# Router logits as seven differences to expert 7, with a PSUM bank of its own for each group of a tile

## What is computed

```
logits = (h @ router_w.T + router_b).reshape(T, O, E)        # T=4096, O=512, E=8
probs = softmax(logits, axis=-1)
w, sel = top_k(probs, 2);  w = w / sum(w)
c[t, e] += w summed over the features o for which sel picks e   # .at[t_idx, sel].add(w)
expert_out = einsum('th,eoh->teo', h, expert_w) + expert_b
final = einsum('te,teo->to', c, expert_out)
x = x + final
```

## Time and profile before

| | |
|---|---|
| median of 3 runs | 2307.93 us (2307.9 to 2308.26) |
| span of the profiled execution, from its first to its last instruction | 2306.4 us |
| PE busy | 2285.2 us, 99% |
| DVE busy | 1682.9 us, 73% |
| ACT busy | 1145.2 us, 50% |
| POOL busy | 11.3 us |
| last tile's groups to the first matmul of the second expert tile | 1583.8 to 1628.3 us |

### The profile page before, as it was taken

The page is one execution under the profiler, slowest core; times in us unless marked ns, Lnnn a source line. Parts: engine busy times, 40 slices in busy tenths (PEclk is TensorE's granted clock), DMA queues, the critical chain, the costliest instruction groups (busy, mean ns, idle before and its releaser), DMA issues.

```text
span 2306.4 us, 29968 instructions
## 1 busy us (share of the span) xinstructions
PE 2285.2 (99%) x10201; PEld 1881.0 (82%) x10201; DVE 1682.9 (73%) x2522; ACT 1145.2 (50%) x1686; POOL 11.3 (0%) x20
## 2 busy tenths in 40 slices
PE   7999999999999999999999999999999999999999
PEld 5777888888888887888888888888888888888887
DVE  8985444444434346888899999998988888888883
ACT  7754333232323235788888888888422222222221
POOL 0000000000000000000000000000000000000000
PEclk9999999999999999999999999999999999999999
DMA  6314212122121317211111212115322222222220
GB/s 206 105 42 139 76 37 75 55 56 75 37 86 26 91 37 255 73 57 66 59 64 64 78 55 77 61 58 199 134 96 82 77 95 79 80 95 76 83 82 23
DMA packets 154026, 191.04 MB, mean 83 GB/s; under 512 B 62898, under 2 KB 96242, under 8 KB 151666
## 3 DMA queue, kind: packets, MB, share of 16 engines
q1 hardware_dynamic: 110690, 135.26, 18.1%
q10 hardware_dynamic: 43152, 55.06, 7.3%
q0 software_dynamic: 128, 0.07, 0.0%
HBM read 129.01 MB, written 61.34 MB: 83 GB/s over the span
## 4 chain that ended last, share of the span: by engine, by line
PE 89%; issue 5%; DVE 4%; ACT 2%; DMA 0%; ACTq 0%; POOLq 0%; POOL 0%; DVEq 0%; SPq 0%
PE slot L1599 16%; PE plane L1749 10%; PE plane L1747 10%; PE plane L1745 10%; PE ex L1785 10%; PE ex L1787 10%; PE ex L1786 10%; PE pj L1612 7%; PE slot L1661 3%; PE slot L1568 1%; PE slot L1650 1%; DVE cols L1238 1%; DVE ew_lo L1478 1%; ACT x1t_hi L795 0%; PE slot L1578 0%
## 5 line engine op out<-in xcount | busy, mean ns | idle before, releaser
L1599 PE MATMUL slot<-y_hi,wgu 128*128 128x512 f32 x1024 | 402.6, 393 | 1.4 <-DVE y_lo L1118 0.7
L1599 PE MATMUL slot<-y_lo,wgu 128*128 128x512 f32 x1024 | 399.8, 390 | 0.0
L1745 PE MATMUL plane<-rw_hi,hb 128*128 128x512 f32 x1008 | 392.2, 389 | 0.0
L1749 PE MATMUL plane<-rw_lo,hb 128*128 128x512 f32 x1008 | 392.1, 389 | 0.0
L1747 PE MATMUL plane<-rw_hi,hb 128*128 128x512 f32 x1008 | 392.1, 389 | 0.0
L1785 PE MATMUL ex<-ew_hi,hb 128*128 128x512 f32 x992 | 386.0, 389 | 0.2 <-ACT ex L1056 0.2
L1787 PE MATMUL ex<-ew_lo,hb 128*128 128x512 f32 x992 | 385.9, 389 | 0.0
L1786 PE MATMUL ex<-ew_hi,hb 128*128 128x512 f32 x992 | 385.9, 389 | 0.0
L1056 ACT ACTIVATE ex<-eb_sb 128x512 f32<-128x512 f32 x248 | 149.0, 602 | 448.9 <-DVE acc L1507 385.8
L1453 DVE SCALAR_TENSOR_TENSOR lead_in<-code_in,wts 128x1024 bf16<-128x1024 bf16 x256 | 311.4, 1216 | 1.2
L1599 PEld LDWEIGHTS slot<-y_hi,wgu 128*128 128x128 f32 x1024 | 192.8, 188 | 45.5 <-DVE q_scale L1125 2.9
(11 more groups left out here) (164 smaller groups left out, 3213.6 us busy)
## 6 DMA issues: line engine op xcount, KB each, us to landing
hb<-h_scratch SPq DMA_DIRECT2D x34, 512.0 KB, 3.3
code_scratch<-half_code SPq DMA_DIRECT2D x64, 256.0 KB, 2.0
half_in<-code_scratch SPq DMA_DIRECT2D x32, 512.0 KB, 3.4
hb<-h_scratch ACTq DMA_DIRECT2D x30, 512.0 KB, 3.7
h_scratch<-ht ACTq DMA_DIRECT2D x48, 256.0 KB, 2.9
q_raw<-in_w_ffn SPq DMA_DIRECT2D x21, 512.0 KB, 3.5
x_scratch<-x_res ACTq DMA_DIRECT2D x8, 1024.0 KB, 4.3
rraw<-in_rwT SPq DMA_DIRECT2D x8, 1024.0 KB, 9.2
```

The source lines that it names most:

```text
L1599: last = mm(slot[s % 2][:, g, :], wgu[:, c, r * P:(r + 1) * P], y[:, c, :], start=(c == 0 and v == 0), stop=(c == DC - 1 and v == 1))
L1745: mm(bank[:, :, :], hb[:, u, c, 0, :], rw_hi[:, w, c, o], start=False, stop=False, skip_group_check=True)
L1749: last = mm(bank[:, :, :], hb[:, u, c, 0, :], rw_lo[:, w, c, o], start=False, stop=True, skip_group_check=True)
```

## The change

The router's weights and biases become differences: plane q holds expert `LOADED[q]` minus expert 7. The eighth logit is then zero and is neither multiplied, nor evacuated, nor stored.

- GpSimd makes the seven difference planes in the middle blocks of stage 1 (`gaps`): 28 steps, each a DMA in, a subtraction of 128x512, and a DMA out to `gap_dram`, five steps after each `power(i)`; and the bias differences in three instructions before `power(7)`. SP loads the seven planes from `gap_dram` once all 28 are out.
- A tile has `PT = 7` groups. Groups 0 to 2 and 4 to 6 are pairs of planes for a half; group 3 is the seventh plane with both halves in one bank. Each group has its own bank (`plane` 0 to 3, `spare` 0 to 2), seeded for the next tile right after its evacuation.
- `half` now works on planes 1 to 6 in pairs of three, and takes the seventh plane (`side`) and zero in with `scalar_tensor_tensor`: 14 steps (`KT`) for 12. Its first steps for s = 0 wait for three evacuations, the fifth for the fourth. The last subtraction is one instruction over seven planes. `stand` takes the sign of seven planes and, in a second instruction, that of minus the second logit.
- Between the stages, raw experts 6 and 7 are loaded as soon as SP is past tile 29; the last tile's groups go in the order `LAST_GROUPS`, the splits in the order `SPLITS`; ACT's list has `stand(30, 1)` before the first `split_expert`; expert 7's high part takes the place of raw expert 6, so its split waits for `elo` of expert 6. One `split_router` and one router load fall away.

```diff
...
-PT = 8
-KT = 12
+PT = 7
+KT = 14
 KD = 2
 EPS = 1.1920928955078125e-07
 SCALE_FLOOR = 1.0011717677116394e-08
 
 
+NQ = E - 1
+LOADED = [0, 1, 4, 5, 2, 6, 3, 7]
+HOME = [(1, 3), (4, 6), (3, 7)]
+SIDE = [0, 7]
+PLACES = [[3, 0, 1, 2, 4, 5, 6, 7], [0, 1, 2, 4, 5, 6, 3, 7]]
+
 UW = 2 * D
 STEP = [128.0, 32.0, 8.0, 2.0]
+LAST_GROUPS = [0, 4, 1, 5, 2, 6, 3]
+SPLITS = [0, 1, 2, 3, 6, 4, 5, 7]
...
+            sp.wait_ge(gap_out, 16 * NQ * DC)
             sp.dma_start(bias_sb[:, :, :, :], rb).then_inc(braw_in, 16)
             sp.wait_ge(drained, use(NBLK - 1, f"gu{HC - 1}")[0] + 1)
-            for e in range(E):
-                sp.dma_start(rraw[:, e, :, :].rearrange("p c o -> p (c o)"), rwT[e]).then_inc(rraw_in[e], 16)
+            for e in range(NQ):
+                sp.dma_start(rraw[:, e, :, :].rearrange("p c o -> p (c o)"), gap_dram[e]).then_inc(rraw_in[e], 16)
...
+            load_expert(6)
+            load_expert(7)
             sp.wait_ge(plane_filled, (NT - 1) * PT)
             load_h(0, 0)
-            for b in range(4):
+            for b in range(3):
                 sp.wait_ge(plane_filled, (NT - 1) * PT + 2 * (b + 1))
-                for e in (2 * b, 2 * b + 1):
-                    sp.dma_start(eraw[:, e, :, :].rearrange("p c o -> p (c o)"), ewT[e]).then_inc(eraw_in[e], 16)
+                load_expert(2 * b)
+                load_expert(2 * b + 1)
...
+            def gaps(count):
+
+                for t in range(step[0], min(step[0] + count, NQ * DC)):
+                    c, q = t // NQ, t % NQ
+                    at = slice(c * D, (c + 1) * D)
+                    if q == 0:
+                        if c:
+                            pool.wait_ge(gap_done, t)
+                        pool.dma_start(ref_rows, rwT[NQ][:, at]).then_inc(gap_ref, 16)
+                    if t:
+                        pool.wait_ge(gap_out, 16 * t)
+                    pool.dma_start(rows, rwT[q][:, at]).then_inc(gap_in, 16)
+                    pool.wait_ge(gap_ref, 16 * (c + 1))
+                    pool.wait_ge(gap_in, 16 * (t + 1))
+                    nc.gpsimd.tensor_tensor(rows, rows, ref_rows, ALU.subtract).then_inc(gap_done, 1)
+                    pool.wait_ge(gap_done, t + 1)
+                    pool.dma_start(gap_dram[q][:, at], rows).then_inc(gap_out, 16)
+                step[0] += count
+
             power(0)
-            with pool.Fori(1, NBLK - 1) as i:
+            for i in range(1, NBLK - 1):
                 power(i)
+                gaps(5)
+            pool.wait_ge(braw_in, 16)
+            ref_bias = bias_sb[:, PT, :, :]
+            for s in range(2):
+                at = bias_sb[:, 4 * s:4 * s + 3, :, :].rearrange("p b e n -> p (b e) n")
+                nc.gpsimd.tensor_tensor(at, at, ref_bias[:, s, :].unsqueeze(1).to_broadcast([P, 6, HO]),
+                                        ALU.subtract).then_inc(bias_gap, 1)
+            nc.gpsimd.tensor_tensor(bias_sb[:, 3, :, :], bias_sb[:, 3, :, :], ref_bias, ALU.subtract).then_inc(bias_gap, 1)
...
+            act.wait_ge(drained, l1_use(NBLK - 1, "h1")[0] + 1)
+            for g in range(4, PT):
+                seed(g)
...
+            def evacuate(n, s, u):
+
+                for g in range(4 * s, 4 if s == 0 else PT):
+                    act.wait_ge(plane_filled, n * PT + (g + 1))
+                    nc.scalar.activation(logits_at(g, u), bank_of(g)[:, :, :], ACT.Copy).then_inc(evac, 1)
+                    act.wait_ge(evac, n * PT + (g + 1))
+                    seed(g)
...
+            def stand(n, s, u, second=None):
 
                 act.wait_ge(tour, n * (2 * KT) + (s + 1) * KT)
                 if not isinstance(n, int) or n * 2 + s > 1:
                     act.wait_ge(joined, n * 2 + (s - 1))
-                flat = L[:, s, :, :].rearrange("p e n -> p (e n)")
-                nc.scalar.activation(sgn[:, s, :], flat, ACT.Sign).then_inc(signs, 1)
-                act.wait_ge(signs, n * 2 + (s + 1))
+                flat = L[:, s, u:u + NQ, :].rearrange("p e n -> p (e n)")
+                second = m2[:, s, :] if second is None else second
+                nc.scalar.activation(sgn[:, s, 0:NQ * HO], flat, ACT.Sign).then_inc(signs, 1)
+                nc.scalar.activation(sgn[:, s, NQ * HO:E * HO], second, ACT.Sign, scale=-1.0).then_inc(signs, 1)
+                act.wait_ge(signs, n * 4 + 2 * (s + 1))
...
+                if e == E - 1:
+                    act.wait_ge(elo, SPLITS.index(6) + 1)
+                nc.scalar.activation(ew_hi(e), raw_expert(e), ACT.Copy).then_inc(ehi, 1)
+
+            evacuate_last(0)
+            stand(NT - 2, 1, 0)
+            evacuate_last(1)
             split_expert(0)
+            evacuate_last(2)
             split_expert(1)
-            stand(NT - 2, 1)
-            evacuate_last(0, 2)
-            evacuate_last(0, 3)
-            evacuate_last(1, 0)
-            evacuate_last(1, 1)
+            evacuate_last(3)
+            evacuate_last(4)
             split_expert(2)
-            evacuate_last(1, 2)
-            split_expert(3)
-            evacuate_last(1, 3)
-            for e in range(4, E):
+            evacuate_last(5)
+            evacuate_last(6)
+            for e in SPLITS[3:]:
                 split_expert(e)
-            stand(NT - 1, 0)
+            stand(NT - 1, 0, 1)
...
 
-                dve.wait_ge(evac, n * PT + 4 * (s + 1))
-                step(tt(top4, L[:, s, 0:4, :], L[:, s, 4:8, :], ALU.max))
-                step(tt(low4, L[:, s, 0:4, :], L[:, s, 4:8, :], ALU.min))
+                last = isinstance(n, int) and n == NT - 1
+                dve.wait_ge(evac, n * PT + (PT if s else LAST_GROUPS.index(2) + 1 if last else 3))
+                step(tt(top3, L[:, s, 1:4, :], L[:, s, 4:7, :], ALU.max))
+                step(tt(low3, L[:, s, 1:4, :], L[:, s, 4:7, :], ALU.min))
                 after(1)
-                step(tt(top2, top4[:, 0:2, :], top4[:, 2:4, :], ALU.max))
+                step(tt(top2[:, 0, :], top3[:, 0, :], top3[:, 2, :], ALU.max))
                 after(2)
-                step(tt(low4[:, 0:2, :], low4[:, 0:2, :], low4[:, 2:4, :], ALU.max))
-                step(tt(top4[:, 0:2, :], top4[:, 0:2, :], top4[:, 2:4, :], ALU.min))
+                step(tt(low3[:, 0, :], low3[:, 0, :], low3[:, 2, :], ALU.max))
+                if s == 0:
+                    dve.wait_ge(evac, n * PT + (LAST_GROUPS.index(3) + 1 if last else 4))
+                step(stt(top2[:, 1, :], side, 0.0, top3[:, 1, :], ALU.max, ALU.max))
+                step(stt(low3[:, 1, :], side, 0.0, low3[:, 1, :], ALU.min, ALU.max))
                 after(3)
+                step(tt(top3[:, 0, :], top3[:, 0, :], top3[:, 2, :], ALU.min))
+                after(5)
+                step(stt(top3[:, 1, :], side, 0.0, top3[:, 1, :], ALU.max, ALU.min))
                 step(tt(m1, top2[:, 0, :], top2[:, 1, :], ALU.max))
-                after(5)
-                step(tt(low4[:, 0:2, :], low4[:, 0:2, :], top4[:, 0:2, :], ALU.max))
                 step(tt(m2, top2[:, 0, :], top2[:, 1, :], ALU.min))
-                after(7)
-                step(tt(low4[:, 0, :], low4[:, 0, :], low4[:, 1, :], ALU.max))
-                after(9)
-                step(tt(m2, m2, low4[:, 0, :], ALU.max))
+                after(8)
+                step(tt(low3[:, 0:2, :], low3[:, 0:2, :], top3[:, 0:2, :], ALU.max))
+                after(11)
+                step(tt(low3[:, 0, :], low3[:, 0, :], low3[:, 1, :], ALU.max))
+                after(12)
+                step(tt(m2, m2, low3[:, 0, :], ALU.max))
                 if joins:
                     join(n if s else n - 1, 1 - s)
-                after(10)
-                step(tt(L[:, s, 0:4, :], L[:, s, 0:4, :], m2.unsqueeze(1).to_broadcast([P, 4, HO]), ALU.subtract))
-                step(tt(L[:, s, 4:8, :], L[:, s, 4:8, :], m2.unsqueeze(1).to_broadcast([P, 4, HO]), ALU.subtract))
+                after(13)
+                step(tt(L[:, s, u:u + NQ, :], L[:, s, u:u + NQ, :], m2.unsqueeze(1).to_broadcast([P, NQ, HO]), ALU.subtract))
...
-            for b in range(4):
-                group(NT - 1, 1, NT // 2 - 1, 0, b)
-                group(NT - 1, 1, NT // 2 - 1, 1, b, bank=spare[b])
+            for g in LAST_GROUPS:
+                group(NT - 1, 1, NT // 2 - 1, g)
...
-                        pe.wait_ge(evac, NT * PT - 3 + e)
-                    pe.wait_ge(ehi, e + 1)
+                    if e != 3:
+                        pe.wait_ge(evac, (NT - 1) * PT + LAST_GROUPS.index((e + 4) % E) + 1)
+                    pe.wait_ge(ehi, SPLITS.index(e) + 1)
                     for c in range(DC):
...
```

More of the change, by code:

```diff
@@ L247, in build @@
         ht = sb("ht", [P, 2, 2, BLK], F32R, pa)
+        last_rows = sb("last_rows", [P, D], F32, pa)
         slot = [pb(f"slot{s}", [P, 2, BLK], pa) for s in range(2)]
@@ L352, in build @@
         w_done = sem("w_done")
-        rraw_in = [sem(f"rraw_in{e}") for e in range(E)]
+        gap_ref = sem("gap_ref")
+        gap_in = sem("gap_in")
```

(57 more changed lines are left out.)

118 lines of the change are left out of this document (67 added, 51 removed).

## The result

The changed kernel takes **2254.49 us** (median of 4 runs, 2252.87 to 2255.79), the kernel before 2307.91 on the same chip (2306.73 to 2308.26): a ratio of 0.9769, 95% interval 0.9755 to 0.9782. That is 53.4 us, 2.3%, where 58.1 were forecast. The profiled execution took 2252.87 us with a span of 2251.2. Its span is 55.2 us shorter than the span before.

A forecast was written before the change was run, and what follows sets the result against it. PE was taken to bound the kernel, with DVE becoming the bound in tiles 11 to 28. 84.3 us saved on PE, less 26.2 given back, leave 58.1 and a median of 2249.8 us; range 2236 to 2274.

The forecast's parts named there:

- bare half: DVE's router half without a `total`: 14 steps for 12, 8.83 us where it was 9.36.
- the unknown `scalar_tensor_tensor`: In DVE's half: the f32 instruction of 256 columns, absent from the trace, was taken at 0.34 us.
- join wait: Router half: DVE waits 1.2 us for `stand`, gone once DVE lags; rival: it stays in tiles 11 to 28, 2272, chance 0.08.
- The last link: Between the stages: ACT's split of expert 7, done at 1561.1, releases PE's last matmuls of the first expert tile.
- Stage 1 was put at nothing: Stage 1: GpSimd's 28 steps and three bias subtractions cost 0, within bounds of 0 and 45 us.
- end of tile 30's last subtraction: Router's end: DVE starts tile 29 at 1497.0, and four bare halves bring this subtraction to 1532.0.
- from there to the second expert tile's first matmul: Between the stages: a chain over ACT, DVE and PE, 38.2 us, ending at 1570.2.
- median over span: Whole run: the median time was put 1.5 us above the profiled span.
- the 1.2 us of lag: Tile 11: DVE's wait at the join becomes the first part of its lag, once, 1.2 us.
- A fallen clock: PE after its new waits: a granted clock that falls could add 3 to 5 us.
- Full absorption: Rival, router: DVE's lag is absorbed and PE's gain counts in full, 81.3 us, median 2226.7; chance 0.10.
- GpSimd's hold-ups: Rival, stage 1: POOL holds DVE up beyond the slack, one microsecond for each of 28 steps, 2278; chance 0.08.

The follow-up runs named there:

- experiment 1: The changed kernel with DVE's 36 extras in tiles 11 to 28 working on only 8 columns of each half, weights incomplete: 2231.61 us.
- experiment 3: The changed kernel with DVE making the low part of expert 6 before those of 2 and 3: 2250.05 us.
- experiment 8: The changed kernel without GpSimd's 28 `gaps` steps, the seven planes loaded raw, bias subtractions kept: 2253.39 us.
- Experiment 7: The changed kernel with the first two tiles' `weigh` moved ahead of ACT's loop over tiles 3 to 10: 2253.81 us.

## Why the prediction was right, and where it was off

**The steps that held.** DVE and PE were forecast rightly, and with them nearly the whole time. PE does one group less a tile, and in tiles 3 to 10 it has no gap. The bare half is 8.83 us by the profile and 8.83 by the sum, the period with a `total` 9.97, just as forecast; the unknown `scalar_tensor_tensor` cost what was taken for it. DVE became the bound in tiles 11 to 28, and experiment 1 prices that at 22.9 us by the times and 24.4 by the profiles. There is no join wait once DVE lags: the 12.2 us that DVE waits at L1452 lie in 930 to 1120 us, where PE paces and they are free, and between 1120 and 1165 there are only 0.3. PE waits for seeds from tile 22 on, as forecast, and for expert 7's split (4.86 us) between the stages. The last link is the one foreseen, as experiment 3 shows by taking 4.4 us off it.

**The step that was wrong.** Stage 1 was put at nothing because a hold-up of 1.0 to 1.6 us fits the slack of 2.5, and the bias subtractions because they had the rest of block 7. The slack was read at one chunk. At the first chunk of a block it is 0.48 us, and a bias subtraction holds DVE for over 3 us. So hold-ups do reach PE, by chance of timing: 0 to 3.2 us of stage 1 in the profiles (experiment 8). That the profile after shows a stage 1 of the old length was luck of that execution. The error is small beside the 53.4 us.

**What was mis-sized**, 4.7 us in all, three small terms:

| term | forecast | measured |
|---|---|---|
| end of tile 30's last subtraction | 1532.0 | 1533.4 |
| from there to the second expert tile's first matmul | 38.2 | 39.7 |
| median over span | 1.5 | 3.3 |

The first is most likely the `weigh` at tile 11: a table load and four sigmoids stand in ACT's order before its evacuations. I read DVE's wait of 2.54 us there as the 1.2 us of lag that the prediction booked at tile 11, and 1.3 more. DVE's start of tile 29 agrees: 1498.4 where 1497.0 was forecast. The prediction's list of what stands before tile 11 left these instructions out. Experiment 7 agrees in its trace and is not decided by its time.

The second is PE's clock. The eight matmuls of expert 7's high part come behind a wait of 4.86 us and take 3.27 us start to start, where 8 x 0.2267 = 1.81 were counted. The granted clock of that stretch (first row) was 0.66 on the mean, so part of it ran at the lower level of 1.2 GHz, after the engine had stood idle; then it is back at 2.4 GHz:

```profile
1561.00:1566.00 5.00, 3.47 (x9) 2.85 (x10) 5.00 (x3) 4.97 (x6) 0.00 (x0) 0.66 0.00 0
1566.00:1573.00 7.00, 7.00 (x32) 5.79 (x31) 6.07 (x8) 4.49 (x8) 0.00 (x0) 1.00 0.12 39
```

A fallen clock had been named as 3 to 5 us on the slow side, but left out of the sum. It cost 1.5, since the matmuls behind the longer wait of 5.98 us (the `spare` bank at 1521.86) lay off the path: ACT, which evacuates them, waits for no group of the last tile. The third comes from setting the median beside the span of one execution: the profiled one, 2252.87 us, was the fastest of the four, 1.6 us under their median. How much of that is hold-ups in stage 1 stays open, as the other three left no trace.

**The rivals.** Full absorption (2226.7) needed DVE not to be the bound; experiment 1 shows what the kernel does then, 2231.6. In its profile tile 30's last half starts 608.0 us after the router's first matmul, which is what this rival had reckoned; the rest of the difference is that profile's late router and the slower stretch behind it. Join waits (2272) didn't come. GpSimd's hold-ups were there (below), and some went beyond the slack, but they cost 1 to 3 us and not 28. A step of `gaps` took 8 to 13 us: in one block five of them fill 348 to 392 us, 44 of its 109, far from 21.8 us a step.

## What to carry to other kernels

When a change relieves the bound engine in a stage where a second one is 98% busy, sum both engines' work for the stage: the larger sum sets the new pace, and here about 23 of 84 us went to DVE's excess. Then look at where the second engine's deferrable work stands; spreading it over stretches in which that engine still has room gave back 11 to 12 us and reordering by what releases the last link 4 more. A hold-up's slack must be read at every place where the held engine meets the bound one, the tightest above all, and not at the most frequent: here 0.48 us at a block's first chunk and none at its end, beside 2.5 at most others. And where such a hold-up comes and goes with timing, one profile against one can miss it; several profiles of the same stage showed it.
